# Moving the w3, w4 and bias-row loads of a recommender kernel behind the first tile's gathers

## The reference

```
fm    = emb_table[arange(26)[None, :], cat_idx]           # 512 x 26 x 128
dense = relu(relu(relu(x @ Wd1 + bd1) @ Wd2 + bd2) @ Wdf + bdf)
Z     = concatenate([fm, dense[:, None, :]], axis=1)      # 512 x 27 x 128
S     = einsum('bie,bje->bij', Z, Z)
x     = concatenate([S[:, iu, ju], dense], axis=-1)       # 512 x (351 + 128)
x     = relu(x @ Wt1 + bt1)                               # 1024
x     = relu(x @ Wt2 + bt2)                               # 1024
x     = relu(x @ Wt3 + bt3)                               # 512
x     = relu(x @ Wt4 + bt4)                               # 256
out   = sigmoid(x @ Wo + bo)
```

## Time and profile before

| | us |
|---|---|
| median of 3 runs (lowest, highest) | 197.6 (197.54, 198.29) |
| the profiled execution, whole | 197.5 |
| its span in the profile | 195.7 |
| TensorE busy in it | 161.7 (83%) |
| POOL busy | 105.0 (54%) |
| VectorE busy | 64.3 (33%) |
| ScalarE busy | 49.1 (25%) |

### The profile page before, as it was taken

How to read it: one execution, slowest core, us unless ns; L and a number is a source line. 1 busy time by engine, 2 the same in 40 slices (tenths; PEclk the granted TensorE clock), 3 DMA queues, 4 the chain that set the end, 5 groups by cost and what they waited for, 6 DMA issues and landing times.

```text
span 195.7 us, 3866 instructions
## 1 busy us (share of the span) xinstructions
PE 161.7 (83%) x1745; PEld 124.3 (64%) x1745; DVE 64.3 (33%) x91; ACT 49.1 (25%) x79; POOL 105.0 (54%) x111
## 2 busy tenths in 40 slices
PE   2999995126149999996999998799899779999983
PEld 1334431014139988874898886699788568988852
DVE  3032704423144542320536140352613133422211
ACT  3355679104025212011231110133111013111110
POOL 3787877878777787777777777777400000000000
PEclk9999999755555999999699999999999999999999
DMA  3998878699734333244443334343300000000000
GB/s 93 323 265 253 268 217 249 169 259 304 231 53 57 53 48 55 53 54 54 55 57 57 54 50 56 55 55 54 48 0 0 3 3 3 0 0 0 0 3 0
DMA packets 8323, 17.68 MB, mean 90 GB/s; under 512 B 2677, under 2 KB 3961, under 8 KB 8178
## 3 DMA queue, kind: packets, MB, share of 16 engines
q0 software_dynamic: 3328, 6.82, 22.4%
q1 hardware_dynamic: 4978, 10.60, 16.8%
HBM read 17.41 MB, written 0.00 MB: 89 GB/s over the span
## 4 chain that ended last, share of the span: by engine, by line
PE 67%; POOL 14%; issue 10%; DMA 4%; DVE 2%; ACT 1%; DVEq 0%
PE mp L401 23%; POOL rows L281 14%; PE tp L368 12%; PE mp L424 11%; PE gp L344 7%; PE gp L333 5%; PE mp L436 4%; DMA rows<-in_emb,row_of 3%; PE tp L381 2%; PE gp L357 1%; DMA idx<-in_cat_idx 1%; DVE xb L622 1%; DVE zt L616 1%; PE gp L381 0%; DVE z L655 0%
## 5 line engine op out<-in xcount | busy, mean ns | idle before, releaser
L281 POOL DMA_INDIRECT rows<-in_emb,row_of x104 | 104.2, 1001 | 33.9 <-issue 30.8
L333 PE MATMUL gp<-ident,rows 128*128 128x128 f32 x104 | 17.7, 295 | 11.5 <-DMA rows<-in_emb,row_of 11.4
L368 PE MATMUL tp<-xt,w 117*128 117x128 f32 x192 | 26.5, 292 | 0.7 <-ACT xt L509 0.7
L401 PE MATMUL mp<-w2h,a1h 128*128 128x512 f32 x64 | 26.0, 407 | 0.7 <-DVE z L655 0.7
L368 PEld LDWEIGHTS tp<-xt,w 117*128 117x128 f32 x192 | 25.0, 206 | 1.5 <-issue 0.9
L401 PE MATMUL mp<-w2l,a1h 128*128 128x512 f32 x64 | 25.6, 400 | 0.0
L401 PE MATMUL mp<-w2h,a1l 128*128 128x512 f32 x64 | 25.4, 398 | 0.0
L333 PEld LDWEIGHTS gp<-ident,rows 128*128 128x128 f32 x104 | 13.8, 153 | 15.9 <-DMA rows<-in_emb,row_of 13.2
L344 PE MATMUL gp<-zt 128*32 128x27 f32 x1024 | 13.6, 205 | 11.7 <-issue 10.8
L344 PEld LDWEIGHTS gp<-zt 128*32 128x32 f32 x1024 | 11.9, 120 | 14.6 <-issue 13.7
L616 DVE COPY zt<-gp 128x512 f32<-128x512 f32 x12 | 12.6, 1047 | 17.7 <-PE gp L333 17.7
(11 more groups left out here) (64 smaller groups left out, 158.9 us busy)
## 6 DMA issues: line engine op xcount, KB each, us to landing
w<-in_wt SPq DMA_DIRECT2D x13, 512.0 KB, 4.8
rows<-in_emb,row_of POOLq DMA_INDIRECT x104, 3.4
w<-in_wt SPq DMA_DIRECT2D x3, 468.0 KB
bc<-in_rows SPq DMA_DIRECT2D x1, 1024.0 KB, 11.2
wd_sb<-in_wd SPq DMA_DIRECT2D x1, 512.0 KB, 3.2
w1d<-in_wt SPq DMA_DIRECT2D x1, 512.0 KB, 5.5
wdf_sb<-in_wdf SPq DMA_DIRECT2D x1, 128.0 KB, 3.2
idx<-in_cat_idx SPq DMA_DIRECT2D x1, 52.0 KB, 2.1
```

Of the source, the lines that this page charges most:

```text
L281: pool.indirect_dma_start(out=rows[:, n % RING, :], out_offset=None, in_=emb.rearrange("c v e -> (c v) e"), in_offset=bass.IndirectOffsetO ...
L333: last = pe.transpose(gp[:, 2 + g % 2, n * P:(n + 1) * P], rows[:, (N_CAT * t + f0 + n) % RING, :], ident[:])
L368: last = pe.matmul(tp[:, m // 4, (m % 4) * P:(m % 4 + 1) * P], w1[0:PC, k, m * P:(m + 1) * P], xt[0:PC, k, :], start=(k == 0), stop=(k == ...
L401: last = pe.matmul(mp[:, h, :], a[:, k, :], w[:, k, cols], start=(k == 0 and part == 0), stop=(k == M1 - 1 and part == 2))
```

## The change

SP waits, after the w1 loads, for the last group of tile 0's gathers. Then it issues the four w3 loads, each after the one before has landed, and w4 and the bias rows right behind the last. ScalarE's and VectorE's four w3 splits each come after the first tile's pair copies; two of the four used to come before them.

```diff
--- before.py
+++ after.py
@@ -255,8 +255,10 @@
                 else:
                     sp.wait_ge(w1_in[0], 16)
                 sp.dma_start(w1[0:PC, c, :], wt1[c * PC:(c + 1) * PC, :]).then_inc(w1_in[c], 16)
+            sp.wait_ge(gathered[0][NG - 1], 16 * Z_GROUPS[NG - 1][1])
             for n in range(M1, SPLIT_LOADS):
-                sp.wait_ge(w1_in[2] if n < M1 + 2 else w_in[n - 2], 16)
+                if n > M1:
+                    sp.wait_ge(w_in[n - 1], 16)
                 load_to_split(n)
             sp.dma_start(w4[:], wt4.rearrange("(k p) n -> p k n", p=P)).then_inc(w4_in, 16)
             sp.dma_start(bc[:], bass.AP(tensor=rows_in.tensor, offset=rows_in.offset, ap=[[0, P], [1, N_ROWS]])).then_inc(rows_sem, 16)
@@ -549,11 +551,9 @@
             split_hi(7)
             features(0, 4)
             features(0, 6)
-            split_hi(M1)
-            split_hi(M1 + 1)
             pairs_out(0)
-            split_hi(M1 + 2)
-            split_hi(M1 + 3)
+            for n in range(M1, SPLIT_LOADS):
+                split_hi(n)
 
             for t in range(TILES - 1):
                 for m in range(M1):
@@ -665,11 +665,9 @@
             features(0, 3)
             split_lo(7)
             features(0, 5)
-            split_lo(M1)
-            split_lo(M1 + 1)
             turn_sums(0)
-            split_lo(M1 + 2)
-            split_lo(M1 + 3)
+            for n in range(M1, SPLIT_LOADS):
+                split_lo(n)
             ve.wait_ge(rows_sem, 16)
             for t in range(TILES - 1):
                 for m in range(M1):
```

## The result

The changed kernel took 203.39 us (median of 4 runs, 201.13 to 204.97) beside 197.94 us for the kernel before (4 runs, 197.54 to 200.7): a ratio of 1.019, interval 1.012 to 1.026. Ratios here compare only those executions of each kernel that lie within 1.5% of its fastest, while medians are of all, so the two medians alone would give 1.028. The change is slower, and outside the range of 194.0 to 200.6. The profiled execution took 201.95 us, with a span of 200.1, against 197.5 and 195.7 before. The time of both kernels varies from run to run: in the three later comparisons the kernel before took 194.2 to 203.2 us (53 executions, medians 197.7, 197.4 and 197.7).

A forecast was written before the change was run, and what follows sets the result against it. Bound by POOL's gather issue until 40 us, TensorE from 58.83. Of 4.0 us won up to layer 1, 2.9 go into a hole before layer 2, leaving 1.05: 197.5 - 1.05 = 196.45, given as 196.5; range 194.0 to 200.6.

The forecast's parts named there:

- Step 1: Tile 0's last gather, flying without SP's loads, takes 3.5 us instead of 5.22 and lands at 43.4, 1.7 us sooner.
- Step 2: TensorE's stand in tile 0's grams shrinks from 4.67 to 2.4 us; layer 1 begins at 54.8, 4.0 us sooner.
- Step 3: SP's w3 loads take 3.7 us each, so the bias rows are issued at 55.4 and land at 64.4.
- Step 4: VectorE's wait for the bias rows holds its copy and sum; layer 2 effectively begins at 66.8, with 1.05 us left.
- break-even of 65.4: Landing time of the bias rows, before layer 2, at which the change would neither win nor lose.
- C: Rival, slower: bias rows land at 68.4, layer 2 begins at 70.8, 3.0 us late, 200.5 us in all; chance 0.22.
- D: Rival: after the hole, layer 2 runs 3 us at half clock, losing 1.5 us, 197.9 in all; chance 0.24.
- 1.5 us of cover: ScalarE's copy after its w3 casts ends at 60.6, before TensorE wants that bank at 62.1 in layer 1.

The follow-up runs named there:

- e8_change_again: The changed kernel unaltered, measured again: 201.41 us, ratio 1.017 to the kernel before.
- e4_no_gather_wait: The changed kernel without SP's wait for the gathers, one w3 load at a time from the end of the w1 loads: 195.35 us, ratio 0.996.
- e7_chain_free_late: The changed kernel without SP's gather wait, VectorE's bias-row wait at first use, last two w3 splits of both engines behind layer 1's relus: 195.61 us, ratio 0.984.
- e11_tail_spread: e7_chain_free_late with the bias rows waiting for the fourth w3 load and w4 for the bias rows: 192.74 us, ratio 0.975.
- e6_hole_half_filled: The changed kernel with two more fp32 products of 512 columns on TensorE before layer 2 of tile 0: 201.77 us, ratio 1.014.
- e1_wait_late: The changed kernel with VectorE's wait for the bias rows moved to the layer 2 sum that first uses them: 197.82 us, no ratio given.
- e10_rows_first: The changed kernel with the bias rows issued straight after the gather wait, ahead of the w3 loads: 204.64 us, ratio 1.037.
- e5_wait_splits_late: The changed kernel with VectorE's bias-row wait at first use and both engines' last two w3 splits behind layer 1's relus: 197.26 us, ratio 0.993.

## Why the prediction was wrong, point by point

**Step 1, right.** The last gather took 3.76 us against 3.5 foretold, and 3.4 to 3.7 in the other gated kernels. It was issued 0.7 us later in this execution, so it landed at 44.3, not 43.4; in e8_change_again it landed at 42.7.

**Step 2, right in kind.** A stand of 2.65 us (2.4 foretold), 3.58 in the second profile. Layer 1 at 56.15, foretold 54.8. What the step took over unseen is the length of layer 1: 9.04 us before, 10.1 now, on the lower clock for longer. TensorE alone was ready at 66.3, not 63.9, so of the 4.0 us that were to be won up to layer 2 it could have kept 1.6 at most in this execution, even with the bias rows in time.

**Step 3, the step that failed: the time of a w3 load on its own.** The kind of path was right and the term was too small. The three w3 loads took 44.36 to 58.16, 13.8 us, where 3 x 3.7 = 11.1 was put down: 4.6 each, above even the 4.3 that I took as the upper bound. I reasoned that a load without another behind it must be quicker. In the gated chains it was not: 4.4 to 5.2 us. In the three kernels whose chain begins earlier (e4_no_gather_wait, e7_chain_free_late, e11_tail_spread) it took 3.6 to 4.6. Packets in the changed kernel (packets, MB, time share): SP's queue from 46 to 47 us and from 47 to 48, then all that moved from 49 to 50, the gathers' queue alone:

```profile
q1 hardware_dynamic: 89, 0.18, 50.5%
q1 hardware_dynamic: 131, 0.25, 66.6%
...
q0 software_dynamic: 25, 0.06, 74.0%
```

In the fullest us of each of these three loads 0.23 to 0.29 MB pass, in e8_change_again up to 0.35, against the 0.40 of the earlier trace rows with several under way. And SP's queue then moves nothing for a while: the second load, issued at 48.77, has 0.01 MB moved by 51 us. So for nearly half of that load hardly a byte moves; what fills that time no run here shows. The other terms: bias rows issued 1.87 us after the fourth load instead of 0.93 (w4's issue alone took 1.42), and 8.0 us to land against 9.0. In sum 0.96 from the gather, 2.7 from the loads, 0.94 from the issues, less 0.96: 3.6 us late, bias rows at 68.07 instead of 64.4. The 0.96 is mostly the chance of this execution; in e8_change_again the last gather was 0.7 us early, the loads took 14.5 us, and the rows were in at 67.6 all the same. The figure of the Trainium skill (DMA: Bandwidth & Descriptors, section Anatomy of one DMA), from which I estimated 3.2 us, was further off; no w3 load beside gathers here was that quick. That fit is given for DMAs that GpSimd issues, and these are issued by SP, which the prediction did not say. The rule in that page's section Rules for kernel authors, to issue early and wait late, would have pointed to the right sign.

**Step 4, right.** From the bias rows to the first product of layer 2 it took 2.36, 2.36 and 2.27 us (the changed kernel twice, e6_hole_half_filled), where 2.2 was foretold; the wait for the low half came to 0.3, foretold 0.2. The break-even of 65.4 therefore decided.

**The rivals.** C, given 0.22, had the mechanism and the place: bias rows at 68.4, layer 2 at 70.8, against 68.07 and 70.43. D, given 0.24, happened as well, and on top of C. I had made them exclusive, though a later layer 2 is a longer hole: the clock fell in those of 4.1 and 4.2 us and not in e1_wait_late, where TensorE stood 1.38 us in layer 1 and 0.94 before layer 2. C and D together are 200.5 + 1.5 = 202.0, and the profile says 201.95. That the two meet so closely is luck: 3.0 and 1.5 were foretold, 2.56 and 2.61 came, and 0.8 was given back. That case had no chance of its own and lay above the range. The clock's own price was put at 1.5 us and was some 2.3 in the first half of layer 2 (2.61 less the 0.3 above): layer 2 ran on it for 5.7 us, not 3.

**What was covered.** ScalarE's casts were said to have 1.5 us of cover. The cover was used up: the fourth load landed at 62.7, not 59.0, and in e8_change_again TensorE already waited 0.37 us for ScalarE's copy. e10_rows_first shows the price when it is gone.

## What to carry to other kernels

A load that is moved back must be followed to every wait on it, and the wait to all that stands behind it on its engine: here the bias rows were first used at 79.4, 11 us after they had landed even in the slow version, but a wait placed ahead of a loop stopped work that did not need them. Loads held back let the last gather land in 3.4 to 3.8 us instead of 5.2, and one load at a time cut TensorE's stand in the grams. But it gives up much of the rate: 0.5 MB each 4.6 us is 0.11 MB per us, where the queue had moved up to 0.40. Such a chain is better started early than gated. And when a delay opens a hole on TensorE, count the lower clock behind it in the same case, not as another.

## What was not expected of the hardware

A single 512 KB load beside a stream of gathers took 3.6 to 5.2 us, in most cases no less than the 4.3 us of one with another right behind it in the kernel before. SP's issue of w4 right behind the last load of a serial chain took 1.28 to 1.57 us in seven of nine profiles (0.47 in e4_no_gather_wait and in e10_rows_first), against 0.48 before; no run here says why. A gather issued right behind w4 and the bias rows, 1.5 MB, took 9.7 us (e5_wait_splits_late) against 3.5. The granted clock fell in the later tiles in one or two places, differing between profiles of near-identical kernels.
